# Two-layer transformer kernel on one core: linear attention's first two pairs normalised, transposed and multiplied within the feed-forward's last steps, and GpSimd's feed-forward list in another order

## The chip, the cores and the metric

One core of a Trainium2 chip (trn2) runs the whole program in one launch. The metric is device time in microseconds (us) of one execution; less is better. Engines are named as in the profile: PE (TensorE matmuls), PEld (TensorE weight loads), DVE (VectorE), ACT (ScalarE), POOL (GpSimd), SP (SyncE). Each engine works through its own list of instructions in order, and semaphores hold an instruction until what it needs is there.

## The reference

Sixteen sequences of 128 tokens with 128 features pass a transformer block (attention and a gated feed-forward, both modulated by a condition vector), and then a linear-attention block. What matters here is the end of the first and the start of the second:

```python
h2 = modulate(rmsnorm(x, norm2_w), sh_mlp, sc_mlp)
ff = jax.nn.silu(h2 @ w1.T) * (h2 @ w3.T) @ w2.T
x = x + g_mlp * ff                                   # end of block one
...
xn = layer_norm(x, norm_g, norm_b)                   # start of block two
q = (xn @ Wq + bq).reshape(B, T, H, dh)
k = (xn @ Wk + bk).reshape(B, T, H, dh)
v = (xn @ Wv + bv).reshape(B, T, H, dh)
```

## The kernel before

All five engine programs are written out by hand as lists, one function for each engine. Attention (steps t = 0 to 17, one sequence each) ends near 124 us of the trace. The feed-forward and the linear attention then work on pairs of sequences (UNIT = 2, U = 8 pairs, B = 16).

**Feed-forward, step t = 0 to 7.** On PE a step is `b_first(t)`: the product back with w2 for pair t, first of three chunks (L893), and the hidden products of pair t+2, chunk 0 (L881 with w1, L882 with w3); `b_input(t+3)`: the two transposes of pair t+3 (L860); `b_rest(t)`: back chunks 1 and 2, hidden chunks 1 and 2. ACT does a tanh for each hidden chunk (`th`, L587) and the modulated copy of the transposed pair. DVE gates each chunk (`yg` L685, then `ff` L692), multiplies the result of pair t by the gate (`fg`, L701), and takes mean and variance (`bn` L711, `mv` L715). DVE adds the residual itself for pairs 6 and 7 (L727).

**GpSimd's list** (`blocks_gpsimd`, loop over u = 3 to 7) does, per turn: `rms1(u+2)` (two columns of sums, then the power -0.5: L503, L505), `normed1(u)` (the normalised pair `xs2`, which PE transposes: L511), `after_feed_forward(u-3)` (the residual `x2`: L518), `std2(u-5)` (the second norm's 1/std: L526, L528). `rms1(7)` needs the sum of squares of the last sequence, which ACT makes late (`squared`, L1338).

**Linear attention**, units 0 to 8 (seven pairs, then single sequences), one `c_step(t)` per turn on PE and DVE. Its start for unit u: POOL normalises (`xs3`, L571), PE transposes into bank 7 (L930), the copy `hT3` brings it to SBUF (ACT for units 0 and 1: L618, L639; DVE from 2 on: L801), PE multiplies for queries and values (L1015, with bias L1016, into bank 5) and for keys (L985, into bank 6). Then DVE takes the keys' maximum (`kmax` L806, `knb` L818), ACT the exponential (`kx` L624). In the program before, PE's loop calls `c_step(0)` after feed-forward step 6 and `c_step(1)` after step 7; in each of them the transposes come just ahead of what needs them, and the last back product (pair 7) stands behind `c_step(0)`.

Of the kernel before, what the change touches and what calls it, by code (L numbers as in the profile page):

```python
# [32 lines left out]
B, T, D = 16, 128, 128  # L33
# [79 lines left out]
def dit_then_linear_attention(nc, x, cond, pos, norm1_w, qkv_w, q_norm_w, k_norm_w, proj_w, proj_b,  # L113
# [3 lines left out]
    with ctx:  # L117
# [360 lines left out]
        def blocks_gpsimd(g, start=None):  # L478
            q = nc.gpsimd

            def wide(t_, u):
                return t_[:, pair(u)].unsqueeze(2).to_broadcast([128, UNIT, D])

            def split_biases():

                g.wait_ge(pv_v, V_BIAS)
                q.tensor_copy(bias_high[:, :], bias_qvo[:, :]).then_inc(c_bias, 1)
                g.wait_ge(c_bias, 1)
                q.tensor_tensor(bias_rest[:, :], bias_qvo[:, :], bias_high[:, :], ALU.subtract).then_inc(c_bias, 1)
                g.wait_ge(c_bias, 2)  # L490
                q.tensor_copy(bias_mid[:, :], bias_rest[:, :]).then_inc(c_bias, 1)
                q.tensor_copy(bias_parts[0:32, :], bias_high[0:32, :]).then_inc(c_bias, 1)
                g.wait_ge(c_bias, 4)
                q.tensor_copy(bias_parts[32:64, :], bias_mid[32:64, :]).then_inc(c_bias, 1)
                g.wait_ge(c_bias, 5)
                q.tensor_tensor(bias_parts[64:96, :], bias_rest[64:96, :], bias_mid[64:96, :], ALU.subtract).then_inc(c_bias, 1)
                g.wait_ge(c_bias, 6)

            def rms1(u):

                cols = pair(u)
                g.wait_ge(s_sq1, UNIT * u + UNIT)
                q.tensor_scalar(ms1[:, cols], ms1[:, cols], 1.0, EPS0, ALU.mult, ALU.add).then_inc(b_ms, 1)  # L503
                g.wait_ge(b_ms, u + 1)
                q.tensor_tensor(rstd1[:, cols], ms1[:, cols], minus_half[:, 0:UNIT], ALU.pow).then_inc(b_rstd, 1)  # L505

            def normed1(u):

                g.wait_ge(b_rstd, u + 1)
                wait(g, b_xsT, u - 1)  # L510
                q.tensor_tensor(xs2[u % 2][:, :, :], x1[:, pair(u), :], wide(rstd1, u), ALU.mult).then_inc(b_xs, 1)  # L511

            def after_feed_forward(u):

                if not is_unit(u):
                    return
                g.wait_ge(b_fg, u + 1)
                q.tensor_tensor(x2[:, pair(u), :], fg[u % 2][:, :, :], x1[:, pair(u), :], ALU.add).then_inc(b_x2, 1)  # L518

            if start is None:  # L520
                return split_biases, rms1, normed1

            def std(u, rows, ready, mv, var, added, rstd, made):

                g.wait_ge(ready, u + 1)
                q.tensor_scalar(var[:, rows], mv[:, rows, 1], 1.0, EPS1, ALU.mult, ALU.add).then_inc(added, 1)  # L526
                g.wait_ge(added, u + 1)
                q.tensor_tensor(rstd[:, rows], var[:, rows], minus_half[:, 0:rows.stop - rows.start], ALU.pow).then_inc(made, 1)  # L528

            def std2(u):  # L530
                if is_unit(u):
                    std(u, pair(u), b_mv, mv2, var2, c_var, rstd2, c_rstd)

            for u in range(start, U):
                if u + 2 < U:
                    rms1(u + 2)
                normed1(u)
                after_feed_forward(u - 3)
                std2(u - 5)
            after_feed_forward(U - 3)  # L540
            std2(U - 5)
            std2(U - 4)

            for t in c_range():
                if 1 <= t <= 3:
                    std2(U - 4 + t)
# [12 lines left out]
                if is_part(u):  # L559
                    g.wait_ge(c_mv, u + 1)  # L560
                    if u < DRAIN:
                        q.tensor_scalar(nmr3[:, c_rows(u)], mv3[:, c_rows(u), 0], -1.0, 0.0, ALU.mult, ALU.add)
                    std(u, c_rows(u), c_mv, mv3, var3, d_var, rstd3, d_rstd)
                    if u < DRAIN:
                        g.wait_ge(d_rstd, u + 1)
                        q.tensor_tensor(nmr3[:, c_rows(u)], nmr3[:, c_rows(u)], rstd3[:, c_rows(u)], ALU.mult).then_inc(d_nmr, 1)
                u = t
                if is_part(u):
                    g.wait_ge(c_rstd, min(u + 1, U))
                    wait(g, c_xsT, u - 1)  # L570
                    q.tensor_tensor(xs3[u % 2][:, 0:c_size(u), :], x2[:, c_rows(u), :], rstd2[:, c_rows(u)].unsqueeze(2).to_broadcast([128, c_size(u), D]), ALU.mult).then_inc(c_xs, 1)  # L571

        def blocks_scalar(a, start=None):
            q = nc.scalar
# [25 lines left out]
            def b_rest(t):  # L600
                tanh(t + 2, 1)
                tanh(t + 2, 2)

            def b_step(t):
                b_first(t)
                b_input(t + 3)
                b_rest(t)
            if start is None:
                return b_first, b_input, b_rest, tanh
# [2 lines left out]

            a.wait_ge(pv_v, V_BIAS)
            for t in c_range():
                u = t
                if u == 0:
                    a.wait_ge(c_xsT, u + 1)
                    q.activation(flat(hT3[u % 2])[:, 0:c_size(u) * T], bank[XC_BANK][:, 0:c_size(u) * T], ACT.Copy).then_inc(c_hT, 1)  # L618
                u = t - 2
                if is_part(u):  # L620
                    a.wait_ge(c_nb, u + 1)
# [6 lines left out]
                if is_part(u):  # L628
# [4 lines left out]
                    n = c_size(u)  # L633
                    q.activation(qvb[u % 2][:, 0:n, 0:2 * D], bank[QV_BANK][:, 0:n * 2 * D].rearrange("p (u f) -> p u f", f=2 * D),
                                 ACT.Copy).then_inc(c_qvb, 1)
                u = t
                if 0 < u < JOIN:
                    a.wait_ge(c_xsT, u + 1)
                    q.activation(flat(hT3[u % 2])[:, 0:c_size(u) * T], bank[XC_BANK][:, 0:c_size(u) * T], ACT.Copy).then_inc(c_hT, 1)  # L639
                u = t - 3  # L640
                if is_part(u):
                    a.wait_ge(c_qxTp, u + 1)
# [205 lines left out]
        def blocks_tensor(e, start=None):  # L848
# [69 lines left out]
                hidden(t + 2, 1)  # L918
                hidden(t + 2, 2)

            def b_step(t):
                b_first(t)
                b_input(t + 3)
                b_rest(t)
            if start is None:
                return b_first, b_input, b_rest, hidden

            def turned_part(u, dst, src, sm):
                for j in range(c_size(u)):
                    last = q.transpose(dst[:, j * 128:(j + 1) * 128], src(j), ident[:, :])  # L930
                last.then_inc(sm, 1)

            def c_step(t):
                u = t - 3
# [24 lines left out]
                if is_part(u):  # L959
# [10 lines left out]
                u = t  # L970
                if is_part(u):
                    e.wait_ge(c_xs, u + 1)
                    if u == 0:
                        e.wait_ge(b_hT, U)
                    wait(e, c_hT, u)
                    turned_part(u, bank[XC_BANK], lambda j: xs3[u % 2][:, j, :], c_xsT)
                u = t - 1
                if is_part(u):
                    e.wait_ge(c_hT, u + 1)
# [17 lines left out]
                if is_part(u):  # L997
# [7 lines left out]
                u = t  # L1005
                if is_part(u):
                    e.wait_ge(c_hT, u + 1)
                    wait(e, c_qvb, u)
                    if u == 0:
                        e.wait_ge(s_x1, B)  # L1010
                        e.wait_ge(c_bias, 6)
                        e.wait_ge(pv_v, V_DONE)
                    for j in range(c_size(u)):
                        dst = bank[QV_BANK][:, j * 2 * D:(j + 1) * 2 * D]
                        q.matmul(dst, hT3[u % 2][:, j, :], linc[:, 0:2, :].rearrange("p c f -> p (c f)"), start=True, stop=False)  # L1015
                        last = q.matmul(dst, share[:, :], bias_parts[:, 0:2 * D], start=False, stop=True)  # L1016
                    last.then_inc(c_qv, 1)

            for t in range(start, U):
                b_step(t)  # L1020
                if t >= U - 2:
                    c_step(t - (U - 2))
            for t in c_range():
                if t >= 2:
                    c_step(t)

# [46 lines left out]
        def _(g):  # L1074
# [175 lines left out]
            for t in range(LAST_POOL):  # L1250
# [19 lines left out]
                if t == B - 2:  # L1270
                    split_biases()
                    rms1(4)
            blocks_gpsimd(g, 3)

# [865 lines left out]
```

## Time and profile before

| | us |
|---|---|
| median of 3 runs (lowest, highest) | 206.55 (205.71, 207.56) |
| the profiled execution's own time | 206.81 |
| its span in the trace | 205.1 |
| busy: PE, DVE, POOL, ACT | 180.1, 163.7, 140.9, 129.9 |

The rows below give microseconds from the span's start. A window's row has its length, the busy time of each engine with the count of instructions, the granted TensorE clock (1.00 is full speed, 2.4 GHz, and 0.50 is 1.2 GHz), and DMA. Ends of matmuls are modelled, so a busy PE is not necessarily PE at its peak.

### The profile page before, as it was taken

The page shows a single profiled execution, that of the slowest core. Times are in us where ns is not written, and L with a number is a line of the kernel's source. Part 1 is how long each engine was busy: PE and PEld are TensorE (multiplying, and loading weights), DVE is VectorE, ACT ScalarE, POOL GpSimd, SP SyncE. Part 2 cuts the span into 40 slices and gives each one's busy share as a digit, 9 for nine tenths or more (in the row PEclk, how much of TensorE's full clock was granted, in tenths as well). Part 3 has the DMA queues.
Part 4 walks back from the last instruction along what each step waited for, and adds up shares of the span by engine and source line. Part 5 has one row for each costly group of instructions (what it writes and reads, how often), then busy time and mean ns, then how long its engine had stood idle before and what let it go on. Part 6 is the DMA issues. An engine that isn't in the chain of part 4 may idle for free.

```text
span 205.1 us, 6095 instructions
## 1 busy us (share of the span) xinstructions
PE 180.1 (88%) x2039; PEld 142.8 (70%) x2039; DVE 163.7 (80%) x495; ACT 129.9 (63%) x379; POOL 140.9 (69%) x333
## 2 busy tenths in 40 slices
PE   2598887997999999999999989979958899999963
PEld 1345565786687777788787779877946677888642
DVE  6799899896989989898886545868791599999882
ACT  1367798776867777786667774434311368999741
POOL 8889798998989797998820752354355337668651
PEclk9999999999999999999999999999995899999999
DMA  5964008700000000000000000000000000010111
GB/s 109 291 161 166 0 10 324 292 3 0 3 3 2 5 5 0 3 5 0 3 3 0 5 3 0 2 3 2 0 2 0 0 3 0 0 32 26 51 51 54
DMA packets 10428, 8.32 MB, mean 41 GB/s; under 512 B 3105, under 2 KB 9886, under 8 KB 9886
## 3 DMA queue, kind: packets, MB, share of 16 engines
q1 hardware_dynamic: 7006, 7.25, 10.5%
q10 hardware_dynamic: 3392, 0.68, 1.6%
q8 instruction: 17, 0.28, 0.5%
q14 instruction: 13, 0.11, 0.2%
HBM read 6.86 MB, written 1.07 MB: 39 GB/s over the span
## 4 chain that ended last, share of the span: by engine, by line
PE 46%; DVE 15%; issue 6%; POOL 4%; ACT 4%; POOLq 0%; ACTq 0%; DVEq 0%
PE bank L1923 5%; PE bank L893 5%; PE bank L2028 5%; PE bank L881 4%; PE bank L882 4%; DVE qkpad L1638 4%; PE bank L1932 3%; PE bank L1015 3%; PE bank L930 2%; PE bank L1973 2%; PE bank L2002 2%; PE bank L1960 2%; POOL rstd L528 1%; PE bank L1948 1%; PE bank L994 1%
## 5 line engine op out<-in xcount | busy, mean ns | idle before, releaser
L1638 DVE TENSOR_REDUCE qkpad<-bank 128x4 f32<-128x512 f32 x64 | 40.9, 682 | 7.9 <-PE bank L1923 7.0
L1329 ACT ACTIVATE probs<-bank 128x512 f32<-128x512 f32 x64 | 34.6, 595 | 17.4 <-PE bank L1932 16.5
L1923 PE MATMUL bank<-kBD,qTs 32*128 32x256 f32 x224 | 31.7, 399 | 3.8 <-DVE qkpad L1638 2.1
L1932 PE MATMUL bank<-qTm,kBD 32*128 32x128 f32 x448 | 32.5, 283 | 0.0
L1932 PEld LDWEIGHTS bank<-qTm,kBD 32*128 32x128 f32 x448 | 27.1, 186 | 0.0
L1923 PEld LDWEIGHTS bank<-kBD,qTs 32*128 32x128 f32 x224 | 19.7, 184 | 9.5 <-DVE qkpad L1638 5.6
L587 ACT ACTIVATE th<-bank 128x256 f32<-128x256 f32 x24 | 9.3, 388 | 14.9 <-PE bank L882 12.1
L2028 PE MATMUL bank<-probs,vpad 128*32 128x128 f32 x512 | 17.3, 276 | 0.0
L2028 PEld LDWEIGHTS bank<-probs,vpad 128*32 128x32 f32 x512 | 12.9, 109 | 5.6 <-ACT probs L1329 5.5
L2002 PE MATMUL bank<-qkvT,hT 128*128 128x384 f32 x32 | 15.3, 571 | 0.5 <-ACT hT L1346 0.5
L1973 PE MATMUL bank<-ident,qkpad 128*128 128x128 f32 x96 | 14.1, 277 | 1.4 <-POOL qkpad L1215 1.1
L518 POOL TENSOR_TENSOR x<-fg,x 128x256 f32<-128x256 f32 x6 | 4.4, 728 | 15.5 <-DVE fg L701 15.5
L1153 POOL TENSOR_TENSOR partner<-qk,rope 128x96 f32<-128x96 f32 x32 | 14.2, 467 | 0.3 <-ACT qk L1371 0.3
L881 PE MATMUL bank<-hT,w1T 128*128 128x256 f32 x48 | 14.3, 380 | 0.0
L882 PE MATMUL bank<-hT,w3T 128*128 128x256 f32 x48 | 14.3, 379 | 0.0
L893 PE MATMUL bank<-w2T,ff 128*128 128x128 f32 x96 | 14.3, 293 | 0.0
L893 PEld LDWEIGHTS bank<-w2T,ff 128*128 128x128 f32 x96 | 13.6, 209 | 0.6 <-issue 0.3
L685 DVE SCALAR_TENSOR_TENSOR yg<-th,bank 128x256 f32<-128x256 f32 x24 | 10.1, 419 | 3.7 <-ACT th L587 3.4
L1973 PEld LDWEIGHTS bank<-ident,qkpad 128*128 128x128 f32 x96 | 10.8, 141 | 3.1 <-POOL qkpad L1215 1.7
L528 POOL TENSOR_TENSOR rstd<-var,minus_half 128x2 f32<-128x2 f32 (+1 forms) x17 | 11.7, 686 | 1.4
L1164 POOL TENSOR_TENSOR rot<-qk,rope 128x256 f32<-128x256 f32 x16 | 11.8, 737 | 0.0
L701 DVE TENSOR_TENSOR fg<-bank,res 128x128 f32<-128x128 f32 x16 | 3.9, 284 | 9.9 <-PE bank L893 9.9
(254 smaller groups left out, 532.3 us busy)
## 6 DMA issues: line engine op xcount, KB each, us to landing
gate<-in_cond_dram SPq DMA_DIRECT2D x1, 1024.0 KB, 4.7
x<-gate_rows SPq DMA_DIRECT2D x1, 1024.0 KB, 4.8
y<-gate_rows SPq DMA_DIRECT2D x1, 1024.0 KB, 6.9
res<-gate_rows SPq DMA_DIRECT2D x1, 1024.0 KB, 10.2
out_dram<-res SPq DMA_DIRECT2D x7, 128.0 KB, 1.8
xin<-in_x_dram ACTq DMA_DIRECT2D x2, 256.0 KB, 5.0
xin<-in_x_dram SPq DMA_DIRECT2D x1, 512.0 KB, 4.8
ada_n<-in_L_cond_ada_w_dram SPq DMA_DIRECT2D x1, 256.0 KB, 5.4
```

The lines of the kernel that those rows point to most:

```text
L528: q.tensor_tensor(rstd[:, rows], var[:, rows], minus_half[:, 0:rows.stop - rows.start], ALU.pow).then_inc(made, 1)
L881: q.matmul(gu_bank(u, c)[:, 0:UNIT * T], w1T[:, c * 128:c * 128 + 128], flat(hT2[u % 2]), start=True, stop=True)
L882: q.matmul(gu_bank(u, c)[:, UNIT * T:], w3T[:, c * 128:c * 128 + 128], flat(hT2[u % 2]), start=True, stop=True).then_inc(b_gu, 1)
L893: last = q.matmul(bank[F_BANK[j]][:, 0:D], ff[u % 2][c][:, j * T:(j + 1) * T], w2T[:, c, :], start=c == 0, stop=c == FC - 1)
L1153: last = q.tensor_tensor(heads(partner[b % 2][:, :, :])[:, :, :, k::2], heads(qk[b % NQK][:, :, :])[:, :, :, 1 - k:ROPE:2], table(b, 1)[:, ...
L1329: q.activation(probs[2 * r + i][:, :, :, :].rearrange("p f a t -> p (f a t)"), exp_bank(t, r, i)[:, :], ACT.Exp, scale=SCALE).then_inc(s_p, 1)
L1638: q.tensor_reduce(out_, score_bank(b, r, i)[:, :].rearrange("p (f a t) -> p f a t", f=2, a=2), X_AXIS, ALU.max, negate=True).then_inc(s_ma ...
L1923: last = q.matmul(bank[S_BANK[i]][:, f * 2 * T:(f + 1) * 2 * T], qTs[b % 2][rows, f, :], kBD[b % NKB][rows, f, :, :].rearrange("p a t -> p ...
L1932: last = q.matmul(bank[E_BANK[i]][:, (2 * f + k) * T:(2 * f + k + 1) * T], kBD[t % NKB][rows, f, k, :], qTm[t % 2][rows, f, :], start=True ...
L1973: last = q.transpose(dst[:, at_ + f * T:at_ + (f + 1) * T], qkpad[b % NKB][:, s, 8 * f:8 * f + 8, :].rearrange("p h d -> p (h d)"), ident[ ...
L2002: q.matmul(front_bank(b)[:, 128:512], hT[b % 2][:, :], qkvT[:, :], start=True, stop=True).then_inc(s_qkv, 1)
L2028: last = q.matmul(bank[O_BANK][32 * c:32 * c + 32, r * T:(r + 1) * T], vpad[b % NVP][:, col:col + VSTEP], probs[2 * r + i][:, f, k, :], st ...
```

## The change

Four things are moved; no arithmetic is added or removed.

1. POOL's feed-forward list: `normed1(u+1)` comes first in the turn, `rms1(u+3)` last; `normed1(3)` and `rms1(5)` move ahead into the attention loop.
2. POOL's products for linear attention: `normed2(0)` and `normed2(1)` go to the ends of turns 6 and 7, `normed2(2)` before the last `std2` calls.
3. PE: the transposes of unit 0 stand inside feed-forward step 5, the query and value products of unit 0 and the transposes of unit 1 after step 6; `c_step(0)` is gone, and `c_step(1)` follows step 7 as before.
4. ACT: the copy of unit 0 (`c_copied(0)`) stands inside its step 5.

```diff
-                if u + 2 < U:
-                    rms1(u + 2)
-                normed1(u)
+                if u + 1 < U:
+                    normed1(u + 1)
                 after_feed_forward(u - 3)
                 std2(u - 5)
+                if u + 3 < U:
+                    rms1(u + 3)
+                normed2(u - (U - 2))
             after_feed_forward(U - 3)
             std2(U - 5)
+            normed2(JOIN)
             std2(U - 4)
...
+            def normed2(u):
...
+                g.wait_ge(c_rstd, min(u + 1, U))
+                wait(g, c_xsT, u - 1)
+                q.tensor_tensor(xs3[u % 2][:, 0:c_size(u), :], x2[:, c_rows(u), :],
+                                rstd2[:, c_rows(u)].unsqueeze(2).to_broadcast([128, c_size(u), D]), ALU.mult).then_inc(c_xs, 1)
...
+            def c_copied(u):
+
+                a.wait_ge(c_xsT, u + 1)
+                q.activation(flat(hT3[u % 2])[:, 0:c_size(u) * T], bank[XC_BANK][:, 0:c_size(u) * T], ACT.Copy).then_inc(c_hT, 1)
...
                 b_input(t + 3)
+                if t == U - 3:
+                    c_copied(0)
                 b_rest(t)
...
+            def c_turned(u):
+
+                e.wait_ge(c_xs, u + 1)
+                if u == 0:
+                    e.wait_ge(b_hT, U)
+                wait(e, c_hT, u)
+                turned_part(u, bank[XC_BANK], lambda j: xs3[u % 2][:, j, :], c_xsT)
...
+            def b_step(t):
+                b_first(t)
+                b_input(t + 3)
+                if t == U - 3:
+                    c_turned(0)
+                b_rest(t)
+                if t == U - 2:
+                    c_queries_values(0)
+                    c_turned(1)
...
             for t in range(start, U):
                 b_step(t)
-                if t >= U - 2:
-                    c_step(t - (U - 2))
             for t in c_range():
-                if t >= 2:
+                if t >= 1:
                     c_step(t)
...
+                if t == B - 1:
+                    normed1(3)
+                    rms1(5)
             blocks_gpsimd(g, 3)
```

Here `c_queries_values(u)` holds the query and value products as they stood in `c_step`. The lists show the order that results; the names are those of the program, with buffer numbers.

PE at the end of the feed-forward before: `ff1_0` to `ff1_2` are the chunks of pairs 5 and 7, `ff0_0` to `ff0_2` those of pair 6, `hT21` is the input of pair 7, `xs30` and `xs31` are linear attention's units 0 and 1.

```order
L882 MATMUL bank1<-hT21,w3T 128x256
L893 MATMUL bank2<-w2T,ff0_0 128x128
L893 MATMUL bank3<-w2T,ff0_0 128x128
...
L893 MATMUL bank3<-w2T,ff0_2 128x128
L930 MATMUL bank7<-ident,xs30 128x128 x2
L1015 MATMUL bank5<-linc,hT30 128x256
...
L893 MATMUL bank2<-w2T,ff1_0 128x128
...
L893 MATMUL bank3<-w2T,ff1_2 128x128
L930 MATMUL bank7<-ident,xs31 128x128 x2
L985 MATMUL bank6<-hT30,linc 128x256
```

The same place now, from feed-forward step 5 on:

```order
L892 MATMUL bank4<-hT21,w3T 128x256
L936 MATMUL bank7<-ident,xs30 128x128 x2
L903 MATMUL bank2<-w2T,ff1_1 128x128
...
L903 MATMUL bank3<-w2T,ff0_2 128x128
L957 MATMUL bank5<-linc,hT30 128x256
...
L936 MATMUL bank7<-ident,xs31 128x128 x2
L903 MATMUL bank2<-w2T,ff1_0 128x128
...
L903 MATMUL bank3<-w2T,ff1_2 128x128
L1018 MATMUL bank6<-hT30,linc 128x256
```

The transposes of `xs30` moved from behind the back product of pair 6 to the middle of step 5, and those of `xs31` from behind the last back product to ahead of it.

POOL before, from the last attention step on; `ms1`, `rstd1`, `xs20` and `xs21` belong to the feed-forward's norm, `fg0` and `fg1` to its result:

```order
L503 TENSOR_SCALAR ms1<-ms1 128x2
L505 TENSOR_TENSOR rstd1<-ms1,minus_half 128x2
L511 TENSOR_TENSOR xs21<-x1,rstd1 128x256
L518 TENSOR_TENSOR x2<-fg0,x1 128x256
L503 TENSOR_SCALAR ms1<-ms1 128x2
L505 TENSOR_TENSOR rstd1<-ms1,minus_half 128x2
L511 TENSOR_TENSOR xs20<-x1,rstd1 128x256
L518 TENSOR_TENSOR x2<-fg1,x1 128x256
L503 TENSOR_SCALAR ms1<-ms1 128x2
L505 TENSOR_TENSOR rstd1<-ms1,minus_half 128x2
L511 TENSOR_TENSOR xs21<-x1,rstd1 128x256
```

POOL now, from the input of pair 4 on:

```order
L511 TENSOR_TENSOR xs20<-x1,rstd1 128x256
L518 TENSOR_TENSOR x2<-fg0,x1 128x256
L503 TENSOR_SCALAR ms1<-ms1 128x2
L505 TENSOR_TENSOR rstd1<-ms1,minus_half 128x2
L511 TENSOR_TENSOR xs21<-x1,rstd1 128x256
L518 TENSOR_TENSOR x2<-fg1,x1 128x256
L503 TENSOR_SCALAR ms1<-ms1 128x2
L505 TENSOR_TENSOR rstd1<-ms1,minus_half 128x2
L511 TENSOR_TENSOR xs20<-x1,rstd1 128x256
```

Each normalised pair (`xs20`, `xs21`) moved ahead of the residual and of the 1/rms of the pair after it: that of pair 5 now stands before the last `ms1` of this list, which is pair 7's.

## Rows read from the trace of the kernel before

**Rows 1.** The page: the span, and the granted TensorE clock in 40 slices.

```profile
span 205.1 us, 6095 instructions
...
PEclk9999999999999999999999999999995899999999
```

**Rows 2.** Waits of PE: line, releaser, total us, times, longest.

```profile
PE bank L930 <- POOL xs L571: 2.4, 1, 2.4
...
PE bank L860 <- POOL xs L511: 1.1, 1, 1.1
```

**Rows 3.** Windows: start:end, length, busy per engine, granted clock, DMA.

```profile
core 0: us, PE busy (x) PEld busy (x) DVE busy (x) ACT busy (x) POOL busy (x), PEclk, DMA share, GB/s
133.35:134.46 1.11, 0.00 (x1) 0.01 (x1) 0.66 (x5) 0.38 (x1) 1.05 (x2) 1.00 0.00 0
138.83:143.20 4.37, 4.37 (x26) 3.71 (x27) 3.55 (x14) 1.96 (x5) 2.21 (x4) 1.00 0.00 0
151.53:153.90 2.37, 0.00 (x1) 0.01 (x1) 2.27 (x13) 0.00 (x0) 1.47 (x3) 1.00 0.01 3
153.90:160.42 6.52, 5.99 (x23) 4.86 (x24) 0.64 (x5) 0.98 (x2) 2.94 (x6) 0.50 0.00 0
...
196.37:200.08 3.71, 1.63 (x14) 1.25 (x13) 3.06 (x8) 0.86 (x3) 2.20 (x4) 1.00 0.11 35
```

**Rows 4.** Chain that ended last, 129 to 149 us: start, us, what.

```profile
129.19 0.22 PE bank L860 x2
...
132.35 0.40 ACT squared L1338 x2
...
133.82 0.60 POOL xs L511
...
134.46 0.44 PE bank L860 x2
...
143.20 0.44 PE bank L860 x2
143.64 0.89 PE bank L893 x8
...
146.71 0.43 PE bank L881 x2
...
147.57 0.91 PE bank L893 x8
```

**Rows 5.** Timeline of feed-forward steps 3 and 4: start, us, engine, what, idle before.

```profile
140.77 0.73 POOL L518 TENSOR_TENSOR x<-fg,x 128x256 f32<-128x256 f32 x1 [1.99 <-DVE fg L701]
...
142.53 0.61 POOL L511 TENSOR_TENSOR xs<-x,rstd 128x256 f32<-128x256 f32 x1
...
143.20 0.20 PEld L860 LDWEIGHTS bank<-ident,xs 128*128 128x128 f32 x2 [0.40 <-POOL xs L511]
```

**Rows 6.** Timeline where the feed-forward meets linear attention.

```profile
148.50 0.49 DVE L701 TENSOR_TENSOR fg<-bank,res 128x128 f32<-128x128 f32 x2 [0.23 <-PE bank L893]
...
154.11 0.25 DVE L715 BATCH_NORM_AGGREGATE mv<-bn 128x2 f32<-128x6 f32 x2
...
160.21 0.49 DVE L701 TENSOR_TENSOR fg<-bank,res 128x128 f32<-128x128 f32 x2 [5.85 <-PE bank L893]
```

**Rows 7.** Line 727, DVE's residual of pairs 6 and 7: ns min/median/max.

```profile
L727 DVE TENSOR_TENSOR x<-fg,x x2: 424/426/428, 152.6 to 160.7; 128x256 f32<-128x256 f32 x2
```

**Rows 8.** Chain that ended last, 162 to 174 us.

```profile
162.63 0.64 ACT kx L624 x2
...
163.40 0.67 PE bank L985 x2
...
164.29 0.43 PE bank L1015 x2
164.72 0.11 PE bank L1016
...
173.50 0.43 PE bank L985 x2
```

More of the change, by code:

```diff
@@ L532, in std2 @@
                     std(u, pair(u), b_mv, mv2, var2, c_var, rstd2, c_rstd)
+            def normed2(u):
+                if not is_part(u):
+                    return
+                g.wait_ge(c_rstd, min(u + 1, U))
+                wait(g, c_xsT, u - 1)
+                q.tensor_tensor(xs3[u % 2][:, 0:c_size(u), :], x2[:, c_rows(u), :],
+                                rstd2[:, c_rows(u)].unsqueeze(2).to_broadcast([128, c_size(u), D]), ALU.mult).then_inc(c_xs, 1)
             for u in range(start, U):
-                if u + 2 < U:
-                    rms1(u + 2)
-                normed1(u)
+                if u + 1 < U:
+                    normed1(u + 1)
                 after_feed_forward(u - 3)
                 std2(u - 5)
+                if u + 3 < U:
+                    rms1(u + 3)
+                normed2(u - (U - 2))
             after_feed_forward(U - 3)
             std2(U - 5)
+            normed2(JOIN)
             std2(U - 4)
@@ L566, in blocks_gpsimd @@
                         q.tensor_tensor(nmr3[:, c_rows(u)], nmr3[:, c_rows(u)], rstd3[:, c_rows(u)], ALU.mult).then_inc(d_nmr, 1)
[L567 to L571, printed above, removed]
+                if t > JOIN:
+                    normed2(t)
         def blocks_scalar(a, start=None):
@@ L614, in blocks_scalar @@
             for t in c_range():
[L615 to L618, printed above, removed]
                 u = t - 2
@@ L635, in blocks_scalar @@
                                  ACT.Copy).then_inc(c_qvb, 1)
[L636 to L639, printed above, removed]
+                if 0 < t < JOIN:
+                    c_copied(t)
                 u = t - 3
@@ L919, in b_rest @@
                 hidden(t + 2, 2)
[L921 to L924, printed above, removed]
             if start is None:
@@ L931, in turned_part, with c_queries_values @@
                 last.then_inc(sm, 1)
+            def c_turned(u):
[4 more added lines that the diff above has]
+                turned_part(u, bank[XC_BANK], lambda j: xs3[u % 2][:, j, :], c_xsT)
+            def c_queries_values(u):
+                e.wait_ge(c_hT, u + 1)
+                wait(e, c_qvb, u)
+                if u == 0:
+                    e.wait_ge(s_x1, B)
+                    e.wait_ge(c_bias, 6)
+                    e.wait_ge(pv_v, V_DONE)
+                for j in range(c_size(u)):
+                    dst = bank[QV_BANK][:, j * 2 * D:(j + 1) * 2 * D]
+                    q.matmul(dst, hT3[u % 2][:, j, :], linc[:, 0:2, :].rearrange("p c f -> p (c f)"), start=True, stop=False)
+                    last = q.matmul(dst, share[:, :], bias_parts[:, 0:2 * D], start=False, stop=True)
+                last.then_inc(c_qv, 1)
+            def b_step(t):
[7 more added lines that the diff above has]
+                    c_turned(1)
             def c_step(t):
@@ L969, in c_step @@
                     last.then_inc(d_op, 1)
[L970 to L976, printed above, removed]
+                if is_part(t) and t >= JOIN:
+                    c_turned(t)
                 u = t - 1
@@ L1004, in c_step @@
                     turned_part(u, bank[KT_BANK], lambda j: kx[u % 2][:, j, :], c_kxTp)
[L1005 to L1017, printed above, removed]
+                if is_part(t) and t > 0:
+                    c_queries_values(t)
             for t in range(start, U):
                 b_step(t)
-                if t >= U - 2:
-                    c_step(t - (U - 2))
             for t in c_range():
-                if t >= 2:
+                if t >= 1:
                     c_step(t)
```

## The prediction

> **What bounds the kernel now.** I read the page's slices first: the granted clock stands at 9 everywhere but in two slices, 5 and 8, near 154 to 164 us of a span of 205.1 [rows 1]. Something empties TensorE there. Then the waits of PE: after attention the two longest on POOL are 2.4 us on the first transposes of linear attention (L930) and 1.1 us on the transposes of a feed-forward pair (L860) [rows 2]. Windows cut at these waits show their price. An ordinary feed-forward step, 138.83 to 143.20, lasts 4.37 us and PE is busy in all of it, so PE sets the pace; DVE has 3.55, POOL 2.21 and ACT 1.96 us of work in it [rows 3]. From 151.53 to 153.90 PE does nothing; after that the clock is at its lower level, 0.50 or 1.2 GHz, for the 6.52 us up to 160.42, in which DVE has 0.64 us of work [rows 3]. So DVE, which carries the end of the feed-forward, stands idle 5.85 us for the last back product before its multiplication at 160.21 [rows 6]. That product had to queue on PE behind unit 0's start: the wait for POOL, transposes, copy, and products at half clock. Everything later hangs on that point: after 160.21 come pair 7's residual and statistics, then the keys' maximum on DVE and the exponential on ACT at 162.63, for which PE's keys of unit 1 at 163.40 wait [rows 6, 8].
>
> **POOL's list.** Pair 5's normalised input stands behind the 1/rms of pair 7, whose last sum of squares ACT delivers only at 132.35 + 0.40; the product then ends near 134.4 and PE starts its transposes at 134.46, after 1.11 us of nothing [rows 3, 4]. Now pair 5's product takes exactly the place in the list that pair 4's had, and pair 4's was there for the transposes at 129.19 [rows 4]. PE is free at 133.35, so four microseconds are in hand: -1.11.
>
> The same move has a smaller effect on each later step. Transposes whose input waits in SBUF cost 0.22 us in the chain (129.19); those at 134.46 and 143.20 cost 0.44, because their first weight load can't be started ahead: the load unit idles 0.40 us for POOL, whose product starts at 142.53, lasts 0.61 and so ends just before PE needs it [rows 4, 5]. In steps 2, 3 and 4 (one row of the two alike at 138.83 and 143.20 stands here) the input is now made a step earlier: -3 x 0.22 = -0.66. Together -1.77 up to the start of step 5. A step then takes 4.15 us, still above DVE's 3.55.
>
> **Unit 0's transposes inside step 5.** They add 0.22 us to PE ahead of pair 5's last back chunks: +0.22. The wait they bring is for POOL's normalised unit. It takes the list place, behind the residual of pair 3 and the 1/std of unit 1, that pair 7's input had: residual at 140.77, product from 142.53, end 143.14 [rows 5]; earlier by the 1.55 gained up to there, 141.6. PE comes to it after the first hidden chunk of pair 7: 146.71 + 2 x 0.43 - 1.77 = 145.80 [rows 4]. So there are 4.2 us of cover (2.7 even if nothing had been gained). Behind the wait on PE stand the rest of step 5's back and hidden products, and behind ACT's copy two tanh; if the cover were gone, each microsecond late would cost one. ACT's copy and POOL's product of 0.61 us go into their idle time in a step, 2.4 and 2.2 us [rows 3]. Unit 1's product comes one step later, at 145.8, and is wanted at 151.1. The new wait of POOL on PE's transposes, ahead of the residuals, is for transposes done a step before; I take it at nothing, and its bounds are 0 and the 1.11 us that the list cost before.
>
> **Where the two stages meet.** Before, pair 5's back product ended at 147.57 + 0.91 = 148.48 [rows 4] and DVE's last multiplication began at 160.21 [rows 6]: 11.73 us. Now it ends at 148.48 - 1.77 + 0.22 = 146.93. From there two queues run side by side.
> - PE, at full clock: hidden chunks 1 and 2 of pair 7, 4 x 0.43 = 1.72 [rows 4]; back of pair 6, three halves of 0.89 = 1.34 [rows 4]; queries and values of unit 0, 2 x (0.43 + 0.11) = 1.08 [rows 8]; unit 1's transposes 0.22; back of pair 7, 1.34. Sum 5.70, end 152.63.
> - DVE: from the multiplication of pair 5 at 148.50 to the end of pair 6's statistics at 154.11 + 0.25 it was busy without a gap, 5.86 us [rows 6]. So it ends at 146.95 + 5.86 = 152.81.
>
> DVE is the later by 0.18 us; that is how much PE may exceed its sum at no cost. The last multiplication starts at 152.81 instead of 160.21: **-7.40 us**, of which 1.77 - 0.22 = 1.55 come from the feed-forward and 11.73 - 5.88 = 5.85 from the meeting. PE's price has a bound of +0.44 if the two moved sets of transposes both cost 0.44 [rows 4]: then 5.92, a loss against DVE's end of 0.26 in all.
>
> One rule of the Trainium skill speaks against DVE's 5.86. In this trace DVE's residual of a pair (L727), which reads two SBUF tensors, took 424 ns once and 428 ns the other time, the first beside POOL's power at 152.6, the second with POOL idle [rows 7]. The Trainium skill's page "GPSIMD Engine Reference", section "1. Specifications", says that GpSimd shares its SBUF interface with VectorE and contends with VectorE instructions of two SBUF inputs. Nor should the moved product of unit 2 meet it: DVE's multiplication of pair 5 starts at 146.95 and takes 0.49 [rows 6], from a residual to such a product's end are 2.37 us [rows 5], which gives 149.8, while L727 starts near 152.6 - 1.55 = 151.05. I leave the sum at -7.40.
>
> **After that point** nothing is gained or lost. The keys' maximum, exponential and unit 1's keys keep their distances to DVE's last multiplication, so unit 1's keys come at 163.40 - 7.40 = 156.00. PE gets there early: from 152.63 it has unit 0's keys 0.43, unit 1's queries and values 1.08 and unit 2's transposes 0.22 [rows 4, 8], until 154.36, and then waits 1.64 us for ACT's exponential. This wait is the new stall, and it lies beside the DVE and ACT chain that sets the time.
>
> **The sum.** The profiled execution took 206.81 us, 1.7 more than its span, and lies 0.26 above the median of 206.55. 206.81 - 7.40 = 199.4; against the median 199.15. I forecast 199.2 us.
>
> **The rivals.**
> - *The clock falls in the new wait.* For it: the 2.37 us of nothing before the half-clock stretch [rows 3]. Against it: 1.11 us without work at 133.35 stayed at 1.00, and so did 196.37 to 200.08, where PE was busy 1.63 of 3.71 us [rows 3]. My 1.64 lies between 1.11 and 2.37, with dense work on both sides. Price: as long at half clock as before, 6.52 us, in which PE does 3.26 us less; where PE bounds linear attention that is +3.26 and 202.4 us, and about half of it if DVE and ACT hide the rest: 200.8.
> - *The feed-forward keeps its pace.* If another loop holds the steps at 4.37, or pair 5's input is late again, the 1.77 is lost in part or whole: up to 200.9 us. For it: POOL's product came just in time in each step, as a loop with its own length would. Against it: no other engine has more than 3.55 of 4.37 us of work [rows 3].
> - *The transposes put into step 5 stop the feed-forward: slower.* POOL is in-order, and unit 0's product stands behind a residual that waits for DVE (1.99 us of idle before it at 140.77 [rows 5]). If unit 0 is over 2.4 us late at 145.80, that is after 148.2 or 6.6 us later than I work out, PE stands as long as it did at 151.53 and the clock falls there. Then the PE work left up to the last back product, 0.22 + 0.89 + 5.70 = 6.81 us, takes twice as long: +6.81 + 2.4 against -7.40 gives 208.4 us. Below 2.4 us of lateness it only takes away its own length.
>
> That the change doesn't move what it says can be left out: the lists show each move.
>
> **How the numbers follow.** Forecast 0.76, its own range 198.4 to 200.2 (above, PE's +0.26 and the 0.66 of exposed loads if they stay; below, the scatter of the runs). Clock in the new wait 0.10; unchanged feed-forward pace 0.10; stop in step 5 0.04. The range 198.2 to 201.8 holds the forecast, the second rival and the cheaper half of the first. Runs of the kernel before spread over 0.9%, so 1% is about what can be told from no change: 2.07 us. The first three cases are all faster by more: 0.95, with 0.01 taken off for their mixtures; the last gives 0.03 slower, and 0.02 lies within 1%.
>
> **What would show it.** Right: no wait of PE on L860 after 129 us; steps of 4.15 us; no idle PE between the hidden chunks of pair 7 and 154.4; the clock at 1.00 from 120 us to the end; the last DVE multiplication near 152.8; a PE wait of some 1.6 us on the exponential. Wrong: a wait of PE at unit 0's transposes or of ACT at its copy, a half-clock stretch near 156, DVE waiting again for the last back product, or a feed-forward step still at 4.37.

## The result and the profile after

The changed kernel takes 200.16 us (median of 4 runs, 199.57 to 200.87) against 206.13 us (205.33 to 207.56) of the kernel before beside it: ratio 0.9705, 95% interval 0.9635 to 0.9775. The forecast was 199.2 us in a range of 198.2 to 201.8. The profiled execution is one of the two longer ones, 200.87 us with a span of 199.0.

The page of the changed kernel, span and granted clock; it answers to [rows 1]:

```profile
span 199.0 us, 6095 instructions
...
PEclk9999999999999999999999999999999999999987
```

The two slices at half clock near 154 to 164 us are gone. At the very end there are now two low digits that the kernel before did not have.

Waits of PE (line, releaser, total us, times, longest), which answers to [rows 2]. Lines after the change: L870 transposes a feed-forward pair (before L860), L936 a unit of linear attention (before L930), L1018 makes keys (before L985).

```profile
PE bank L936 <- DVE xs L837: 2.1, 2, 1.2
...
PE bank L1018 <- ACT kx L636: 1.5, 1, 1.5
```

POOL appears for neither set of transposes any more. The wait for the keys' exponential that the prediction announced is there; the two waits on L837 belong to the last units, in the tail.

Windows of the changed kernel (columns as in [rows 3]): a feed-forward step; the part in which DVE finishes the feed-forward; DVE's last multiplication up to unit 1's keys; and three pieces of the tail.

```profile
133.57:137.72 4.15, 4.15 (x29) 3.79 (x27) 3.55 (x14) 1.85 (x5) 3.28 (x6) 1.00 0.00 0
...
150.79:153.00 2.21, 2.21 (x18) 1.99 (x17) 2.11 (x13) 0.87 (x2) 1.33 (x4) 1.00 0.01 4
...
153.00:156.19 3.19, 1.71 (x10) 1.16 (x9) 2.90 (x12) 0.77 (x3) 2.85 (x6) 1.00 0.00 0
...
191.00:192.00 1.00, 0.70 (x7) 0.40 (x5) 0.43 (x2) 0.23 (x1) 0.75 (x2) 1.00 0.33 97
192.00:193.00 1.00, 0.12 (x1) 0.13 (x2) 1.00 (x2) 0.00 (x0) 0.72 (x1) 0.83 0.00 0
193.00:196.00 3.00, 3.00 (x15) 2.20 (x15) 0.51 (x3) 0.77 (x2) 0.46 (x1) 0.50 0.15 44
```

The step is 4.15 us instead of 4.37, at the same 3.55 us of DVE work. Between 150.79 and 153.00 PE and DVE are both busy almost throughout, where DVE used to stand idle for 5.85 us. And 193 to 196 us is at 0.50 of the clock.

The timeline of DVE, where the feed-forward meets linear attention (start, us, what, idle before); it answers to [rows 6]:

```profile
126.19 0.49 DVE L711 TENSOR_TENSOR fg<-bank,res 128x128 f32<-128x128 f32 x2 [0.38 <-PE bank L903]
...
147.17 0.49 DVE L711 TENSOR_TENSOR fg<-bank,res 128x128 f32<-128x128 f32 x2 [0.45 <-PE bank L903]
...
153.00 0.49 DVE L711 TENSOR_TENSOR fg<-bank,res 128x128 f32<-128x128 f32 x2
153.53 0.42 DVE L737 TENSOR_TENSOR x<-fg,x 128x256 f32<-128x256 f32 x1
...
154.67 0.39 DVE L816 TENSOR_REDUCE kmax<-bank 128x2 f32<-128x256 f32 x1
```

The three `fg` rows are pairs 0, 5 and 7. In the profile before they stand at 125.97, 148.50 and 160.21 (the last two are in [rows 6]); pair 0 there:

```profile
125.97 0.49 DVE L701 TENSOR_TENSOR fg<-bank,res 128x128 f32<-128x128 f32 x2 [0.38 <-PE bank L893]
```

From pair 0 to pair 5 it was 22.53 us and is 20.98 (-1.55); from pair 5 to pair 7 it was 11.71 and is 5.83 (-5.88). Together -7.43.

The balance of the two spans: the multiplication of pair 0 comes 0.22 later (126.19 against 125.97; in the runs below this start lies anywhere from 125.64 to 126.42), then -7.43; from there to unit 1's keys it is 3.19 us in both traces, and a row far into linear attention (the products with the query features) keeps a distance of 7.21 between the traces from 159.66 to 178.35. Then the tail, seen on PE from the last unit's transposes on. First the window of the kernel before, then PE's timeline of the changed kernel:

```profile
200.08:205.10 5.02, 2.03 (x15) 1.44 (x15) 0.93 (x4) 0.77 (x2) 0.91 (x2) 1.00 0.20 56
```

```profile
190.07 0.33 PE L936 MATMUL bank<-ident,xs 128*128 128x128 f32 x1 [0.90 <-DVE xs L837]
...
192.88 0.48 PE L936 MATMUL bank<-ident,xs 128*128 128x128 f32 x1 [1.18 <-DVE xs L837]
193.14 1.06 PE L866 MATMUL bank<-warm 128*128 128x256 bf16 x4
```

From these transposes to the end it was 5.02 us and is 199.0 - 192.88 = 6.12: the four warming matmuls ahead of the output product take 1.06 us there, and 0.60 in a tail at full clock. So 0.22 - 7.43 + 1.10 = -6.11, and the spans differ by 205.1 - 199.0 = 6.1. The span fell by 1.3 us less than the forecast 7.40; 1.10 of that is the tail, at half clock, and 0.22 the later start.

### The profile page after: what moved, and what is told of

It is laid out like the page before. It is cut to its first block, busy times and chain, and to the rows that moved or that the text cites. A ratio compares the mean times of both kernels' runs of the same rounds, so it can differ in the third digit from the quotient of the medians.

```text
span 199.0 us, 6095 instructions
## 1 busy us (share of the span) xinstructions
PE 177.7 (89%) x2039; PEld 141.8 (71%) x2039; DVE 163.4 (82%) x495; ACT 129.2 (65%) x379; POOL 141.2 (71%) x333
## 4 chain that ended last, share of the span: by engine, by line
PE 45%; DVE 17%; issue 6%; ACT 3%; POOL 3%; POOLq 0%; ACTq 0%; DVEq 0%
PE bank L1946 5%; PE bank L2051 5%; PE bank L891 5%; PE bank L892 5%; DVE qkpad L1661 5%; PE bank L903 4%; PE bank L1955 3%; PE bank L936 2%; PE bank L957 2%; PE bank L2025 2%; PE bank L1996 1%; PE bank L1983 1%; PE bank L1971 1%; PE bank L1027 1%; POOL rstd L528 1%
## 5 line engine op out<-in xcount | busy, mean ns | idle before, releaser
L903 PE MATMUL bank<-w2T,ff 128*128 128x128 f32 x96 | 13.1, 276 | 0.0
L903 PEld LDWEIGHTS bank<-w2T,ff 128*128 128x128 f32 x96 | 12.2, 192 | 0.3
L1235 POOL TENSOR_TENSOR qkpad<-rot,ny 128x256 f32<-128x256 f32 x15 | 9.7, 648 | 2.2 <-DVE ny L1758 0.4
```

The source lines that it names most:

```text
L903: last = q.matmul(bank[F_BANK[j]][:, 0:D], ff[u % 2][c][:, j * T:(j + 1) * T], w2T[:, c, :], start=c == 0, stop=c == FC - 1)
```

## Experiments

**POOL's list alone.** The kernel before, with the first of the four moves only:

```diff
             for u in range(start, U):
-                if u + 2 < U:
-                    rms1(u + 2)
-                normed1(u)
+                if u + 1 < U:
+                    normed1(u + 1)
                 after_feed_forward(u - 3)
                 std2(u - 5)
+                if u + 3 < U:
+                    rms1(u + 3)
```

(and `normed1(3)`, `rms1(5)` in the attention loop).

> The kernel before with GpSimd's feed-forward list dealt anew and nothing else. By my sum: no wait of PE on L860 after 129 us, feed-forward steps of 4.15 us instead of 4.37, the last DVE multiplication 1.77 us earlier than in the kernel before, the meeting of the two stages as before (PE without work for 2.4 us, then half clock), time about 1.8 us below before. Rival, the meeting is set by something that doesn't move with the feed-forward: the gain is lost there and the time is that of before.

Measured: 205.08 us (10 runs), 1.56 below the kernel before beside it; ratio 0.9939 (0.9905 to 0.9973). DVE's timeline of the profiled run, the shortest of the ten (204.09 us), `fg` of pairs 0, 5 and 7, and windows over the wait where the stages meet:

```profile
125.68 0.49 DVE L702 TENSOR_TENSOR fg<-bank,res 128x128 f32<-128x128 f32 x2 [0.38 <-PE bank L894]
...
146.43 0.49 DVE L702 TENSOR_TENSOR fg<-bank,res 128x128 f32<-128x128 f32 x2 [0.23 <-PE bank L894]
...
155.53 0.49 DVE L702 TENSOR_TENSOR fg<-bank,res 128x128 f32<-128x128 f32 x2 [3.23 <-PE bank L894]
```

```profile
150.00:153.60 3.60, 1.24 (x6) 0.86 (x7) 2.19 (x13) 0.38 (x1) 3.05 (x7) 1.00 0.01 2
153.60:159.00 5.40, 4.40 (x29) 3.34 (x28) 2.90 (x11) 2.04 (x6) 2.91 (x7) 1.00 0.00 0
```

Pair 0 to pair 5 takes 20.75 us, 1.78 less than before: the term of 1.77 stands. The surprise is the rest: PE still waits 2.4 us at the first transposes of linear attention, but in this run the clock stays at 1.00 behind it, and the meeting takes 9.10 us instead of 11.71. In this run the tail was at the lower clock: 195.39 to the end took 6.21 us. A wait of the same length lowers the clock in one run and not in another.

**The moved transposes and products alone.** The changed kernel with POOL's old list:

```diff
             for u in range(start, U):
-                if u + 1 < U:
-                    normed1(u + 1)
+                if u + 2 < U:
+                    rms1(u + 2)
+                normed1(u)
                 after_feed_forward(u - 3)
                 std2(u - 5)
-                if u + 3 < U:
-                    rms1(u + 3)
                 normed2(u - (U - 2))
```

(and without `normed1(3)`, `rms1(5)` in the attention loop).

> The changed kernel with GpSimd's feed-forward list in its old order, so only linear attention's first products, transposes and copies are moved. If the two parts simply add: 5.6 us below before. If they are coupled, as I think: GpSimd's product for unit 0 (0.61 us) now stands ahead of pair 7's normalised input, which came just in time in the kernel before, so PE waits some 0.6 us for it and the 1.1 us wait for pair 5 stays too: about 5.0 us below before.

Measured: 202.15 us, 4.5 below the kernel before, ratio 0.981 (0.9765 to 0.9855). PE's waits:

```profile
PE bank L869 <- POOL xs L511: 1.7, 2, 1.1
```

The stop of 1.1 us at pair 5 is back, and a second one of 0.6 us has come: pair 7's input now stands behind more of POOL's work. `fg` of pairs 0 and 7 are 125.69 and 154.84, so 29.15 us, 5.09 less than before. The list alone gives 1.78 (up to pair 5) and the moves alone 5.09; together they give 7.43, 0.56 more than the sum of the two. The two parts hang together: without the new list the moved products cost POOL a second late input.

**How much of the meeting is the clock.** The kernel before, with 20 warming matmuls in PE's wait of 2.37 us:

```diff
                 if is_part(u):
-                    e.wait_ge(c_xs, u + 1)
                     if u == 0:
                         e.wait_ge(b_hT, U)
+                        e.wait_ge(warmed, 1)
+                        for _ in range(20):
+                            q.matmul(bank[XC_BANK][:, 0:256], warm[:, 0:128], warm[:, 0:256], start=True, stop=True)
+                    e.wait_ge(c_xs, u + 1)
```

> The kernel before with 20 idle-filling matmuls (0.11 us each) on PE between the back product of pair 6 and unit 0's transposes, where it waits 2.37 us for GpSimd. If the clock carries half of what the meeting costs: granted clock 1.00 from 150 to 165 us, last DVE multiplication near 157.3 instead of 160.21, time 2.9 us below before; the other 2.9 us are the order of the work. Rival, the order alone is the cost and the half clock is hidden by waits: no change.

Measured: 204.36 us, 2.3 below the kernel before, ratio 0.9923 (0.9897 to 0.9949). DVE, pairs 5 and 7:

```profile
148.49 0.49 DVE L701 TENSOR_TENSOR fg<-bank,res 128x128 f32<-128x128 f32 x2 [0.23 <-PE bank L893]
...
157.59 0.49 DVE L701 TENSOR_TENSOR fg<-bank,res 128x128 f32<-128x128 f32 x2 [3.24 <-PE bank L893]
```

The meeting takes 9.10 us, exactly as in the first experiment. Of the 5.88 us that the change takes out of it, 11.71 - 9.10 = 2.61 are the half clock, and 9.10 - 5.83 = 3.27 are the moved work, that is POOL's earlier products and the new order of PE's list: DVE still idles 3.24 us for the last back product here, at full clock.

**The tail of the changed kernel.** Eight instead of two warming matmuls ahead of the transposes of the last two units (where an expectation calls them pairs, these single matmuls are meant):

```diff
-                    hold_clock(t, 2)
+                    hold_clock(t, 2 if t < C_UNITS + 3 else 8)
                     e.wait_ge(d_xs, u + 1)
```

> The changed kernel with 8 instead of 2 idle-filling matmuls ahead of the transposes of the last two sequences of linear attention. If the changed kernel's missing 1.2 us is the clock that falls at 192 us of its profile: clock 1.00 up to the last product, span 197.7 in each run, time about 199.5 with less scatter than the 199.57 to 200.87 of the changed kernel. Rival, it was lost between 157 and 190 us: the time stays 200.2.

Measured: 199.66 us (199.57 to 199.81, 4 runs), ratio 0.9682 (0.9643 to 0.9721). PE in the tail:

```profile
191.43 1.04 PE L866 MATMUL bank<-warm 128*128 128x256 bf16 x8
192.99 0.33 PE L936 MATMUL bank<-ident,xs 128*128 128x128 f32 x1 [0.53 <-DVE xs L837]
193.16 0.60 PE L866 MATMUL bank<-warm 128*128 128x256 bf16 x4
```

The transposes come 0.11 us later than in the changed kernel, the span ends 1.0 earlier (198.0): the tail takes 5.01 us. The half clock of the tail is thus what the profiled run of the changed kernel lost there. That the eight matmuls prevent it is not shown: of the nine profiles here with two matmuls only two have a tail at the lower clock (the changed kernel and the list alone), of the four with eight none. The intervals of the two kernels' ratios overlap too, so of the medians nothing follows.

**Control: the same warming in the kernel before.**

> Control for the fourth experiment: the kernel before, with 8 instead of 2 pairs of warming matmuls ahead of the last unit's transposes. In the profiled execution of before the tail stood at full clock already (5.02 us from the last transposes to the end of the span). Theory (what the eight matmuls gave the changed kernel is the clock of its tail and nothing else): nothing to gain in a run whose tail is at full clock, so 206.6 us, the kernel before's own median, within 0.5%, and a little less scatter. Rival (the extra matmuls save time in some other way, or cost it): off by 1 us or more at a tail of the same 5.0 us.

Measured: 204.86 us (4 runs), ratio 0.9897 (0.9831 to 0.9962), against the theory. The tail was as expected; the difference lies at the meeting, which the tail's matmuls come long after. DVE, pairs 5 and 7, and PE's clock:

```profile
148.16 0.49 DVE L701 TENSOR_TENSOR fg<-bank,res 128x128 f32<-128x128 f32 x2 [0.23 <-PE bank L893]
...
158.91 0.49 DVE L701 TENSOR_TENSOR fg<-bank,res 128x128 f32<-128x128 f32 x2 [4.88 <-PE bank L893]
```

```profile
153.50:155.00 1.50, 0.91 (x4) 0.59 (x5) 0.49 (x4) 0.38 (x1) 1.33 (x4) 0.91 0.00 0
155.00:156.00 1.00, 1.00 (x4) 0.65 (x3) 0.00 (x0) 0.00 (x0) 0.83 (x3) 0.50 0.00 0
156.00:157.00 1.00, 1.00 (x5) 0.71 (x4) 0.00 (x0) 0.11 (x1) 0.78 (x2) 0.50 0.00 0
157.00:158.00 1.00, 1.00 (x7) 1.00 (x6) 0.00 (x0) 0.49 (x1) 0.00 (x0) 0.50 0.00 0
158.00:159.00 1.00, 1.00 (x10) 1.00 (x10) 0.09 (x1) 0.00 (x0) 0.00 (x0) 0.92 0.00 0
```

The half clock held for the three whole microseconds and parts of the two rows beside them (0.09 x 1.5 / 0.5 = 0.27 and 0.08 x 1.0 / 0.5 = 0.16 us), some 3.4 us instead of 6.52, and the meeting took 10.75 us. So the same kernel was run again, with more runs:

> The fifth experiment once more, with more runs: it came out 1% under the kernel before, which the theory (the matmuls give nothing but the tail's clock) did not allow. In its profiled run the tail was as long as before's, and the meeting 1 us shorter since the lower clock ended sooner. Theory (that shorter stretch was a matter of the run, which the tail's matmuls can't reach): over more runs the median comes back to the kernel before's, 206.2 to 206.8 us. Rival (the matmuls in the tail do shorten the time by 1%): 204.9 us again.

Measured: 206.17 us (12 runs), ratio 1.0005 (0.9974 to 1.0036). The 1% did not come back, and the interval leaves no room for the rival; four runs had been too few.

**The cover of unit 0's product.** The changed kernel with extra products on POOL right ahead of it, five in one run and twelve in the other:

```diff
+        late = sem("late")
...
+                if u == U - 2:
+                    g.wait_ge(c_rstd, 2)
+                    g.wait_ge(s_x1, B)
+                    for i in range(5):
+                        wait(g, late, i)
+                        q.tensor_tensor(xin[:, 0:2, :], x2[:, pair(0), :], x1[:, pair(0), :], ALU.mult).then_inc(late, 1)
                 normed2(u - (U - 2))
```

> The changed kernel with five extra products of a pair (some 0.73 us each, one after the other) on GpSimd right ahead of unit 0's normalising product. Its end moves from 141.8 us by about 4 us to 145.8, where TensorE wanted it at 145.86. Theory (4 us of cover): the cover is used up but no more, so TensorE waits 0 to 0.5 us at unit 0's transposes and the time stays within 0.5 us of the changed kernel's 200.2. Rival (the moved list of GpSimd has no room, since what stands behind the product is wanted at once): 2 us or more slower, with waits on the feed-forward's residuals or statistics.

> The same with twelve extra products, so unit 0's product ends some 9 us later, near 151. Theory (cover of 4 us, beyond it each microsecond late stops TensorE): a wait of about 5 us at unit 0's transposes; if the clock stays up the time is 200.2 + 5 = 205.2 us, and if it falls in that wait as it did at 2.4 us in the kernel before, up to 3.3 more, 208.5. Rival (DVE and ACT hide most of the wait, since they are ahead): under 203 us.

Measured: 199.55 us (ratio 0.9658, 0.9609 to 0.9706) with five, 207.5 us (1.0051, 1.0013 to 1.009) with twelve. With five, POOL's and PE's timelines:

```profile
141.09 3.95 POOL L556 TENSOR_TENSOR xin<-x 128x256 f32<-128x256 f32 x5
144.99 0.61 POOL L541 TENSOR_TENSOR xs<-x,rstd 128x256 f32<-128x256 f32 x1
```

```profile
145.66 0.44 PE L943 MATMUL bank<-ident,xs 128*128 128x128 f32 x2
145.94 1.06 PE L910 MATMUL bank<-w2T,ff 128*128 128x128 f32 x8
```

The product ends at 145.60 and PE takes it at 145.66, just in time; up to the next instruction are 0.28 us instead of the changed kernel's 0.22, and `fg` of pair 0 to pair 7 takes 26.90 us instead of 26.81. Four microseconds on POOL cost nothing that can be measured: this is the cover. With twelve, PE's waits and windows of the profiled run:

```profile
PE bank L943 <- POOL xs L541: 5.5, 1, 5.5
```

```profile
145.46:151.10 5.64, 0.17 (x1) 0.00 (x0) 0.83 (x5) 0.38 (x1) 5.17 (x9) 0.95 0.00 0
151.10:153.50 2.40, 2.40 (x11) 2.40 (x12) 0.00 (x0) 0.38 (x1) 2.12 (x4) 0.50 0.00 0
153.50:155.00 1.50, 1.50 (x8) 1.28 (x7) 1.24 (x4) 0.33 (x1) 0.81 (x2) 0.86 0.00 0
```

Pair 0 to pair 7 takes 33.83 us, 7.02 more than in the changed kernel: the 5.64 us of the first window, and 1.38 us for the half clock behind it, which held for 2.40 us and a part of the next row (0.14 x 1.5 / 0.5 = 0.42 us), about 2.8 us in all. That eats the whole gain. The profiled run is the shortest of the ten (206.25 us); the longest took 208.82 at a mean clock of 0.967, where the profiled one has 0.992, so in other runs the clock cost more. The third rival of the prediction was a real mechanism; it only lacked the delay.

**What is last now.** The changed kernel with DVE's two key reductions of unit 0 ahead of pair 7's statistics, and POOL's 1/std of pair 7 behind unit 0's query subtraction:

```diff
-                if 1 <= t <= 3:
+                if 1 <= t <= 2:
                     std2(U - 4 + t)
...
+                if t == 3:
+                    std2(U - 1)
...
                 gated_(t + 2, 2)
+                if t == U - 1:
+                    c_step(1)
                 for u in ((t,) if t >= JOINED + 1 else (t - 1, t) if t == JOINED else (t - 1,)):
...
             for t in range(start, U):
-                if t >= U - 1:
-                    c_step(t - (U - 1))
                 b_step(t)
             for t in c_range():
-                if t >= 1:
+                if t >= 2:
                     c_step(t)
```

> The changed kernel with unit 0's two key reductions on DVE moved ahead of pair 7's statistics, and GpSimd's 1/std of pair 7 moved behind unit 0's query subtraction. It works on what is now last at the meeting: TensorE's wait of 1.5 us for ACT's exponential of unit 0's keys, which hangs on DVE's maximum. Theory (DVE's order sets the time there): the maximum starts some 0.75 us earlier, the wait shrinks to about 0.75 us, and the time falls by up to 0.7, to 199.5 us. Rival (what is put behind is wanted as soon): pair 7's statistics come as much later, unit 3's input with them, and the gain is given back within the next units: 200.2 us.

Measured: 198.85 us, ratio 0.9614 (0.9571 to 0.9656). DVE's and PE's timelines:

```profile
152.63 0.49 DVE L713 TENSOR_TENSOR fg<-bank,res 128x128 f32<-128x128 f32 x2
...
153.50 0.42 DVE L820 TENSOR_REDUCE kmax<-bank 128x2 f32<-128x256 f32 x1
```

```profile
155.04 0.67 PE L1020 MATMUL bank<-hT,linc 128*128 128x256 f32 x2 [0.71 <-ACT kx L638]
...
191.72 0.33 PE L938 MATMUL bank<-ident,xs 128*128 128x128 f32 x1 [1.18 <-DVE xs L841]
```

From the last `fg` to the keys' maximum are 0.87 us instead of 1.67, and PE's wait shrinks from 1.48 to 0.71. Nothing is given back: from the last `fg` to the last unit's transposes are 191.72 - 152.63 = 39.09 us, against 39.88 in the profiled run of the changed kernel (192.88 - 153.00). The gain of 0.79 is still there at that point.

**The best of these, beside the changed kernel.** The last edit and the warmed tail together, and the changed kernel once more on the same chip:

> The eighth and the fourth experiment together: the changed kernel with unit 0's key reductions ahead of pair 7's statistics, and eight instead of two pairs of warming matmuls ahead of the last unit's transposes. Theory (two independent effects, one at the meeting of the stages and one in the tail): the time of the eighth, 198.85, less what it lost in those of its runs whose tail fell, about 0.3 us: 198.6 us, with a scatter of 0.3. Rival (the eighth's runs lost nothing in the tail): 198.85 us, the same.

> The changed kernel itself once more, beside the others, for a comparison on one chip: 199.5 to 200.9 us, in two groups that lie 1.1 us apart (tail at full and at half clock); the ninth experiment beats it by 0.8 to 1.9 us.

Measured, 6 runs each: 198.75 us (198.56 to 199.13; ratio to the kernel before 0.962, 0.9579 to 0.9661) and 199.64 us (199.31 to 200.78; 0.9673, 0.9628 to 0.9718). Every run of the first is below every run of the second; the medians are 0.89 us apart. It is the fastest version here, but whether the warmed tail adds anything to the new order of the keys (198.85 alone) is not decided. The changed kernel's runs fall into two groups again, four at 199.3 to 199.7 and two at 200.5 and 200.8, but here the two longer ones have a mean clock of 1.0 over the span. The run with five extra products has such a one too, 200.58 us at a mean clock of 1.0. What lengthened these three, for which there is no trace, stays open; the tail's clock explains the profiled run, and not necessarily each of the longer runs.

## Why the prediction was right

- **POOL's list, -1.77.** Right: no wait of PE on L870, steps of 4.15 us, and -1.78 where the list was changed alone. Its two parts were told apart well: the chain has L870 at 0.22 us in each step (133.57, 137.72, 141.87), where it had been 0.44.
- **Unit 0's transposes in step 5, +0.22.** Right: -1.77 + 0.22 = -1.55, and -1.55 was measured from pair 0 to pair 5. They wait for nothing; POOL's product ended at 141.82 (forecast 141.6) and PE came at 145.86, 4.0 us of cover instead of 4.2, and the two delays show that this cover is real and ends where it should. POOL's and PE's timelines of the changed kernel, from these products to the end of the meeting:

```profile
141.21 0.61 POOL L540 TENSOR_TENSOR xs<-x,rstd 128x256 f32<-128x256 f32 x1
```

```profile
145.86 0.38 PE L936 MATMUL bank<-ident,xs 128*128 128x128 f32 x2
...
146.97 0.60 PE L891 MATMUL bank<-hT,w1T 128*128 128x256 f32 x2
...
151.39 1.58 PE L903 MATMUL bank<-w2T,ff 128*128 128x128 f32 x12
152.80 0.60 PE L1018 MATMUL bank<-hT,linc 128*128 128x256 f32 x2
```

- **The meeting, 11.73 to 5.88.** Right at 5.83. The term was formed by replacing the whole stretch by two queues, and so needed no split between clock and order; the experiments give it, 2.61 of the clock and 3.27 of the moved work. PE's sum was mis-sized, 5.70 against 5.83 in its timeline (146.97 to 152.80): unit 1's transposes took 0.26 instead of 0.22, and the back product of pair 7 1.41 instead of 1.34. It cost nothing, since DVE was the later by the 0.18 that the prediction had named as the margin. PE has used up most of it: the back product ends at 152.97, and DVE begins at 153.00.
- **DVE's residual beside POOL.** Its two runs in the changed kernel took 425 and 428 ns, so DVE was not held, and the lower sum of 6.79 did not come. The prediction has its two earlier runs the wrong way round: the one at 152.6, beside POOL's power, took 428 ns, and the one with POOL idle 424. These 4 ns were no evidence on a wide product either, since POOL's power works on two columns. What held is the other argument, that none would be beside the residuals: the product of unit 2 ended at 150.12, and they start at 151.28 and 153.53. The last section has wide products that do hold DVE.
- **After that point nothing.** Right up to the tail: unit 1's keys at 156.19 after a wait of 1.48 us (forecast 156.00 and 1.64; PE was 0.13 slower and DVE 0.03 quicker), at a clock of 1.00. The first rival, a fall of the clock in that wait, didn't come. The step that failed is the tail, where the prediction expected 1.00 to the end: there PE waits 0.90 and 1.18 us between small pieces of work, before as after, and in the profiled run the clock fell, +1.10 us. The prediction used a piece of the tail (196.37 to 200.08 at 1.00, [rows 3]) as evidence that such waits leave the clock alone. It was one run's evidence. The forecast has no term for this, and the median of the first comparison lies 0.96 above 199.2. Two of the first four runs, and four of the later six, came within 0.5 us of 199.2.
- **The second and third rivals.** The pace of the feed-forward was not another loop's: it went to 4.15. The stop in step 5 was priced at 6.81 us of clock beside the wait; in the profiled run with twelve extra products the clock part was 1.38, since the half clock ended after some 2.8 us. Its line of 2.4 us, below which the wait would cost only its own length, is not one that the runs show: a wait of that length left the clock at 1.00 in the first experiment.

## What to carry to other kernels

Where an in-order engine carries the end of one stage and the start of the next, write down what each of the two engines has to do from one fixed event on, and forecast the later of the two: that sum was right to 0.05 us, although the stretch it replaced mixed waiting, order and clock. Before moving a producer ahead, work out when it is ready and when it is wanted; the cover is then a number that a delay on the producer can test. And a clock that is up behind a wait in one trace is no proof for the next run: where PE idles between small pieces of work, give both prices.

## What the runs showed of the hardware

- **The clock behind a wait differs from run to run.** A wait of 2.4 us at the first transposes of linear attention left PE at half clock for 6.52 us in the profile of before, for some 3.4 us in the control run, and not at all in the first experiment. Of the runs of the kernel before on one chip, the two at a mean clock of 1.0 took 205.15 and 205.24 us, and those at 0.983 from 205.67 to 207.90: the clock is a part of its scatter. The changed kernel, which has no such wait there, scatters less (1.3 us against 2.2 in the first comparison). The Trainium skill ("TensorE: Matmul & The Clock Gate", "Part 1: The HAM clock gate") says of a kernel's start that the number of matmuls at the lower clock varies from run to run. These runs show such a variation behind a wait in the middle.
- **A matmul whose input comes just in time costs a little more.** The two transposes took 0.28 us up to the next instruction when their input came 0.06 us ahead, and 0.22 when it had been there for 4 us.
- **DVE and POOL do meet, and either can be the one that waits.** The Trainium skill ("GPSIMD Engine Reference", "1. Specifications") states contention between GpSimd and a DVE instruction with two SBUF inputs. Such an instruction is the attention's residual on DVE (L1718). Where nothing of POOL runs beside it, it takes 0.28 or 0.29 us (four times); beside a wide POOL product that began just before, it took up to 0.83, and where it began first the POOL product took 0.85 instead of 0.73. Rows of DVE and of POOL in the changed kernel:

```profile
64.79 0.83 DVE L1718 TENSOR_TENSOR x<-x1g,xin 128x128 f32<-128x128 f32 x1
...
87.81 0.28 DVE L1718 TENSOR_TENSOR x<-x1g,xin 128x128 f32<-128x128 f32 x1
```

```profile
64.74 0.73 POOL L1184 TENSOR_TENSOR rot<-qk,rope 128x256 f32<-128x256 f32 x1
...
87.83 0.85 POOL L1184 TENSOR_TENSOR rot<-qk,rope 128x256 f32<-128x256 f32 x1
...
153.53 0.47 POOL L526 TENSOR_SCALAR var<-mv 128x2 f32<-128x2 f32 x1
```

The last row starts together with DVE's residual of pair 7 (L737 at 153.53) and ends just after it. In every profile in which these two start together (eight of eight) POOL's operation takes 0.47 or 0.48 us instead of 0.19, while the residual keeps its 0.42 to 0.43. POOL's power on two columns beside the residual of pair 6 takes its usual 0.70 us and holds nothing. The rows fit the contention that the Trainium skill states; no run here was made to test it.
